# The maxima's rows of the attention stack: three DMAs for both row tiles instead of six

## The chip, the cores and the metric

The kernel runs on one core of one Trainium2 chip. The metric is the device time of one execution in microseconds (us). Three runs of the kernel before gave 1207.92, 1214.93 and 1221.93 us; the median is 1214.93 us.

## What is computed

One transformer layer on `x` of shape (16, 512, 128): attention with 16 heads of width 8 and an ALiBi bias, then a mixture of eight experts (top 2) plus a shared one, each followed by a layernorm. The change lies in the attention's softmax:

```python
q = (x @ q_w + q_b).reshape(Bx, Tx, NH, HD).transpose(0, 2, 1, 3)
att = jnp.einsum('bhqd,bhkd->bhqk', q, k) * (1.0 / np.sqrt(HD))
att = att + build_alibi_bias(NH, Tx)[None]
att = jnp.where(causal[None, None], att, -jnp.inf)
att = jax.nn.softmax(att, axis=-1)
y = jnp.einsum('bhqk,bhkd->bhqd', att, v)
...
x = _layernorm(x + attention(x)); x = _layernorm(x + ffn(x))
```

## The kernel before, in words

**Two phases.** `attention` runs first, `experts` after it. The change is in `attention`, which takes the 16 sequences of the batch one after the other, as a software pipeline: in step n the unit work of sequence n runs beside the projections of sequence n+2, the maxima of n+1 and n+2, and the output work of n-1.

**The stack.** The scores of a head are a matmul over up to 64 rows of two tiles in SBUF, `qstack` and `kstack` (three buffers of each, 128 partitions, 8 slots of 512 columns). Partitions 0 to 63 are row tile 0, with the even heads, and 64 to 127 row tile 1, with the odd heads. In each row tile, rows 0 to 47 hold q or k cut into bf16 parts, rows 48 to 51 the bias, rows 52 to 54 (`MAX_ROW` and the two after it) minus the row's maximum, cut into three bf16 parts, and the last rows a mask. So the maximum is subtracted by the score matmul itself, and ScalarE takes the exponential straight from PSUM.

**How the maxima's rows are made.** `max_bank` (L601 to L608) computes the scores without the maxima's rows, 40 banks for a sequence, and VectorE reduces each bank (L921). After the last bank of a sequence VectorE gathers the result in `rowmax` (L930, L932). Then, in the last quarter of a step: job `m` transposes `rowmax` on TensorE (L524), ScalarE writes the first part into `mparts[:, 0, :]` (L664, raises `m_high`), and VectorE what is left into `mrest` (L852, raises `m_rest`); job `mr`: ScalarE writes the second part `mparts[:, 1, :]` (`m_high` again), VectorE the third, `mparts[:, 2, :]` (L857, `m_rest` again). `mparts` has 64 partitions, (head, query tile), 32 for each row tile, and 128 queries in a row.

**How they come to the stack.** SyncE waits for all of this (L499, L500) and then issues six DMAs (L504): for row tile 0 the three parts, then for row tile 1 the three parts. Each moves 32 source partitions of 256 bytes into one partition of `qstack`. Those of tile 0 raise `max_rows0`, those of tile 1 `max_rows1`.

**Who waits for them.** In the next step, TensorE's first score unit (unit 0, an even head) waits for `max_rows0` and unit 1 (an odd head) for `max_rows1`. Between the two stands one bank of maxima. ScalarE's job `m` of the next step waits for both before it writes over `mparts`.

**SyncE's order in a step** is fixed: load `xin` for three sequences ahead, load `xres`, 24 DMAs of `parts` into `qstack` and `kstack` (L469, for the sequence two ahead), one DMA that zeroes a piece of `x_sorted` (L493), the maxima's rows (L504), and the store of `x1T` (L509). TensorE's order is written out by `plan`: unit and bank of maxima in turn, with `pv` matmuls and the jobs in between; engines run it in that order.

Of the kernel before, what the change touches and what calls it, by code (L numbers as in the profile page):

```python
# [15 lines left out]
P = 128  # L16
B, T, C = 16, 512, 128
NH, HD = 16, 8
QT = T // P
# [7 lines left out]
PARTS = 3  # L27
ROW_TILES, ROWS, SLOTS = 2, 64, 8
# [316 lines left out]
def attention(nc, io, dram, keep):  # L345

    with ExitStack() as ctx:
# [6 lines left out]
        def sem(name):  # L354
# [50 lines left out]
        names = """const_loaded masks_loaded late_loaded stack_rows_loaded0 stack_rows_loaded1 stack_rows_loaded2 const_ready unit_ready max_ready pv_ready xT_ps q_ps k_ps v_ps m_ps y_ps ynT_ps o_ps  # L405
            x1T_ps lg_ps exp_done xT_ready qk_high y_kept m_high ynT_ready x1T_ready max_taken rowmax_ready
            qk_split m_rest v_ready y_normed z_ready ln_done rstd_ready logits_kept zeros_set vaug_zeroed rows_zeroed masked qk_low res_biased x1_kept x_loaded0 x_loaded1 stats_passed maxima_passed exp_passed
            xres_loaded max_rows0 max_rows1 routed chosen prefix_ps placed places x_scattered ids_set routing_set x1T_stored shared_loaded""".split()
        S = {n: sem(n) for n in names}
        x_loaded = [S["x_loaded0"], S["x_loaded1"]]  # L410
        CONSTS, CONSTS_READY = 16 * 5, 5
# [14 lines left out]
        with nc.Block() as block:  # L426

            @block.sync
            def _(sp):
                def load(done, out, in_):  # L430
                    sp.dma_start(out, in_).then_inc(S[done], 16)

                load("const_loaded", ident[:], io["ident"])
                load("const_loaded", wq[:], io["q_w"])
                load("const_loaded", wkv_in[:], io["kv_w"])
                load("const_loaded", qb[:], io["q_b"].unsqueeze(1))
                load("const_loaded", kb[:], io["kv_b"][0:C].unsqueeze(1))

                def load_later():

                    for n in range(1, STACKS):
                        for stack, rows in ((qstack[n], io["qstack_rows"]), (kstack[n], io["kstack_rows"])):
                            for tile in range(ROW_TILES):
                                load(f"stack_rows_loaded{n}", stack[ROWS * tile + PROD:ROWS * (tile + 1), :, :].bitcast(U16),
                                     rows[tile])
                    load("late_loaded", wo[:], io["o_w"])
                    load("late_loaded", ob[:], io["o_b"].unsqueeze(0).to_broadcast([P, C]))
                    with nc.allow_non_contiguous_dma(reason="the router's weights transposed"):
                        load("late_loaded", gw[:], io["gate_w"].rearrange("e c -> c e"))
                    load("late_loaded", keep["rank"][:], io["rank"].unsqueeze(0).to_broadcast([P, NE]))  # L450
                    load("late_loaded", keep["before"][:].bitcast(U16), io["before"])
                    load("late_loaded", keep["ids"][:], io["ids"])

                def load_stack(st):

                    buffer, done = st.stack(2), stack_loaded[st.stack(2)]
                    if st.number + 2 >= STACKS:
                        sp.wait_ge(S["unit_ready"], st.at(2 - STACKS, SEQ_UNITS, SEQ_UNITS))
                    for part in range(PARTS):
                        for w, (stack, order) in enumerate(((qstack[buffer], Q_PARTS), (kstack[buffer], K_PARTS))):  # L460
                            if part < 2:
                                sp.wait_ge(S["qk_high"], st.at(2, 4, 2 * part + w + 1))
                            else:
                                sp.wait_ge(S["qk_low"], st.at(2, 2, w + 1))
                            for n in range(len(order)):
                                for tile in range(ROW_TILES):
                                    if order[n] == part:
                                        row = ROWS * tile + HD * n
                                        sp.dma_start(stack[row:row + HD, :, :],  # L469
                                                     parts[tile * HD * SLOTS:(tile + 1) * HD * SLOTS, w, part, :]) \  # L470
                                            .then_inc(done, 16)

                def body(st):
                    if st.has(3):
                        if not st.first(3) and (st.every or st.number + 3 >= 2):

                            sp.wait_ge(S["xT_ps"], st.at(1, 1, 1))
                        sp.dma_start(xin[st.par(3)][:], io["x"][bass.ds(st.number + 3, 1)]
                                     .rearrange("b (i p) c -> p (b i) c", p=P)).then_inc(x_loaded[st.par(3)], 16)
                    if st.chained():  # L480
                        if not st.first(-1):
                            sp.wait_ge(S["z_ready"], st.at(-2, 1, 1))
                        sp.dma_start(xres[:], io["x"][bass.ds(st.number - 1, 1)]
                                     .rearrange("b (i p) c -> p (b i) c", p=P)).then_inc(S["xres_loaded"], 16)
                    if st.has(2):
                        load_stack(st)
                    if st.has(0):

                        if st.first(0):
                            sp.wait_ge(S["zeros_set"], 1)  # L490
                        chunk, turn = divmod(st.number * CHUNKS, B)
                        rows = CSLOT * P * CHUNKS // B
                        sp.dma_start(dram["x_sorted"][chunk][turn // CHUNKS * rows:(turn // CHUNKS + 1) * rows, :]  # L493
                                     .rearrange("(n p) c -> p n c", p=P),
                                     zeros[:].unsqueeze(1).to_broadcast([P, rows // P, RW])).then_inc(S["rows_zeroed"], 16)
                    if st.first(2):
                        load_later()
                    if st.has(1):
                        sp.wait_ge(S["m_rest"], st.at(1, 2, 2))  # L499
                        sp.wait_ge(S["m_high"], st.at(1, 2, 2))  # L500
                        for tile in range(ROW_TILES):
                            for a in range(PARTS):
                                row = ROWS * tile + MAX_ROW + a
                                sp.dma_start(qstack[st.stack(1)][row:row + 1, :, :].rearrange("a u (i t) -> a (u i) t", t=P),  # L504
                                             mparts[tile * SLOTS * QT:(tile + 1) * SLOTS * QT, a, :]) \
                                    .then_inc(S[f"max_rows{tile}"], 16)
                    if st.chained():
                        sp.wait_ge(S["x1T_ready"], st.at(-1, 1, 1))
                        sp.dma_start(dram["x1T"][st.number - 1], x1T[:]).then_inc(S["x1T_stored"], 16)  # L509

                steps(sp, body)
                load("shared_loaded", keep["shared_in"][:], io["w_in"][:, NE, :, :])
                load("shared_loaded", keep["shared_down"][:], io["w_down"][:, NE, :, :])
                sp.wait_ge(S["shared_loaded"], 32)
                sp.wait_ge(S["rows_zeroed"], 16 * B)
                sp.wait_ge(S["x1T_stored"], 16 * (B - 1))

            @block.tensor
            def _(pe):
# [91 lines left out]
                def unit(st, g, u):  # L611

                    n = UNITS * g + u
                    if n < ROW_TILES:
                        pe.wait_ge(S[f"max_rows{n}"], st.at(0, 48, 48))
                    if n >= SB or not st.first(0):
                        pe.wait_ge(S["exp_done"], st.at(0, SEQ_UNITS, n - SB + 1))
                    q, ks = qstack[st.stack(0)], kstack[st.stack(0)]
# [43 lines left out]
            def _(act):  # L662
# [3 lines left out]
                def job(st, name):  # L666
# [16 lines left out]
                    elif name == "m":  # L683
                        act.wait_ge(S["m_ps"], st.at(1, 1, 1))
                        if not st.first(1):
                            act.wait_ge(S["max_rows0"], st.at(0, 48, 48))
                            act.wait_ge(S["max_rows1"], st.at(0, 48, 48))
                        copy(mparts[:, 0, :], misc[0:NH * QT, 0:P], "m_high", scale=-1.0)
                    elif name == "mr":
                        act.wait_ge(S["m_rest"], st.at(1, 2, 1))  # L690
                        copy(mparts[:, 1, :], mrest[:], "m_high")
                    elif name == "yn":
                        act.wait_ge(S["ynT_ps"], st.at(-1, 1, 1))
                        if not st.first(-1):
                            act.wait_ge(S["x1T_stored"], st.at(-2, 16, 16))
                        copy(ynT[:], misc[:], "ynT_ready")
                    elif name == "x1t":
                        act.wait_ge(S["x1T_ps"], st.at(-1, 1, 1))
                        copy(x1T[:], misc[:], "x1T_ready")
# [1001 lines left out]
```

## Time and profile before

| what | us |
|---|---|
| median of three runs | 1214.93 |
| profiled execution, its own time | 1221.95 |
| its span, first to last instruction | 1220.2 |
| attention phase, about | 0 to 760 |
| expert phase, about | 760 to 1220 |
| TensorE busy | 1049.4 (86%) |
| VectorE busy | 826.3 (68%) |
| ScalarE busy | 730.3 (60%) |
| GpSimd busy | 695.8 (57%) |

The profile is one execution; times in its views count from its first instruction. In the timeline a row is: start, duration, engine, line of the kernel, operation, output and inputs, how many instructions are merged in the row, and in brackets how long the engine stood idle before it and what ended that wait. "SPq" is SyncE's queue: a row of it is the time in which it issues DMAs, not the time in which they move data.

### The profile page before, as it was taken

What the parts mean: (1) busy time and instruction counts of PE and PEld (TensorE: products, weight loads), DVE (VectorE), ACT (ScalarE), POOL (GpSimd) and SP (SyncE); (2) the same over time, 40 slices, a digit from 0 to 9 for tenths busy, and PEclk for the clock granted to TensorE, in tenths of its full rate; (3) what the DMA queues carried; (4) which work ended last, traced back from release to release, by engine and by line L of the source; (5) the groups of instructions that cost most, each with busy time, mean ns of one, the idle gap of its engine ahead of it and who ended that gap; (6) DMA issues with size and microseconds to landing.
All of it is one profiled execution on the core that took longest, in us unless ns stands there. A gap on an engine that the chain in (4) does not pass through costs nothing. (4 is left out here: it accounts for less than half of the span.)

```text
span 1220.2 us, 28794 instructions
## 1 busy us (share of the span) xinstructions
PE 1049.4 (86%) x9396; PEld 713.9 (59%) x9396; DVE 826.3 (68%) x2070; ACT 730.3 (60%) x1577; POOL 695.8 (57%) x1191
## 2 busy tenths in 40 slices
PE   1577989998989899888888986997999999999991
PEld 0243444444444444344344433787999999999871
DVE  2567788888888888898889832573433334666585
ACT  1116666666667665466666665445777777788542
POOL 1004444554555454377677775377888888788531
PEclk9958999999999998799999998998999999999996
DMA  5734334433453334155334222412223222445233
GB/s 94 77 46 73 59 76 85 73 66 75 77 83 69 73 74 75 44 90 100 78 93 88 59 59 68 191 35 59 79 75 79 74 79 83 116 134 142 89 111 91
DMA packets 124625, 100.42 MB, mean 82 GB/s; under 512 B 19936, under 2 KB 115430, under 8 KB 124034
## 3 DMA queue, kind: packets, MB, share of 16 engines
q1 hardware_dynamic: 114642, 76.49, 31.9%
q0 software_dynamic: 8704, 16.87, 4.2%
q10 hardware_dynamic: 1136, 5.23, 1.3%
q8 instruction: 81, 1.33, 0.5%
q14 instruction: 62, 0.51, 0.2%
HBM read 37.82 MB, written 35.79 MB: 60 GB/s over the span
## 5 line engine op out<-in xcount | busy, mean ns | idle before, releaser
L711 ACT ACTIVATE probs<-scores 128x512 f32<-128x512 f32 x640 | 346.7, 599 | 110.0 <-PE scores L624 108.5
L774 POOL TENSOR_SCALAR_AFFINE_SELECT probs<-probs 128x256 f32<-128x256 f32 (+1 forms) x640 | 235.6, 381 | 255.8 <-ACT probs L711 246.1
L601 PE MATMUL maxed<-kstack,qstack 52*128 52x128 bf16 (+3 forms) x1152 | 224.5, 300 | 70.3 <-DMA kstack<-parts 36.6
L624 PE MATMUL scores<-qstack,kstack 64*128 64x128 bf16 (+3 forms) x1024 | 238.9, 305 | 43.2 <-DMA qstack<-mparts 17.6
L1227 DVE TENSOR_TENSOR e_hid<-e_gate,e_up_ps 128x352 f32<-128x352 f32 (+2 forms) x192 | 107.5, 560 | 184.6 <-ACT e_gate L1506 159.7
L921 DVE TENSOR_REDUCE maxA<-maxed 128x4 f32<-128x512 f32 x256 | 165.5, 682 | 86.4 <-PE maxed L608 85.8
L640 PE MATMUL pv<-probs,vaug 128*32 128x512 f32 (+3 forms) x2048 | 200.1, 464 | 2.9 <-POOL probs L774 2.9
L921 DVE TENSOR_REDUCE maxB<-maxed 128x4 f32<-128x512 f32 x256 | 162.1, 680 | 4.5 <-PE maxed L608 4.4
L1601 POOL DMA_INDIRECT y_tokens<-e_raw,e_row_i x144 | 142.8, 991 | 37.7 <-issue 26.6
L624 PEld LDWEIGHTS scores<-qstack,kstack 64*128 64x128 bf16 x1024 | 75.9, 94 | 150.6 <-ACT probs L711 82.2
L606 PE MATMUL maxed<-causal,halves 64*128 64x256 bf16 (+1 forms) x640 | 160.0, 261 | 0.0
L1506 ACT ACTIVATE e_gate<-e_gate_ps 128x352 f32<-128x352 f32 (+2 forms) x192 | 95.2, 496 | 84.3 <-PE e_gate_ps L1403 47.2
L608 PE MATMUL maxed<-causal,halves 64*128 64x192 bf16 (+1 forms) x640 | 143.8, 228 | 0.0
L601 PEld LDWEIGHTS maxed<-kstack,qstack 52*128 52x128 bf16 x1152 | 75.2, 95 | 91.5 <-issue 40.0
L1468 PE MATMUL e_y_ps<-e_w_down,e_hT 128*128 (+1 forms) x864 | 120.0, 275 | 0.0
L1413 PE MATMUL e_gate_ps<-e_w_in,e_xT 128*128 x432 | 106.3, 354 | 5.0 <-POOL e_w_in L1548 5.0
L1468 PEld LDWEIGHTS e_y_ps<-e_w_down,e_hT 128*128 128x128 f32 (+1 forms) x864 | 107.8, 191 | 0.0
L1413 PE MATMUL e_up_ps<-e_w_in,e_xT 128*128 x432 | 93.5, 325 | 0.0
L921 DVE TENSOR_REDUCE maxC<-maxed 128x4 f32<-128x512 f32 x128 | 82.1, 682 | 0.5
L608 PEld LDWEIGHTS maxed<-causal,halves 64*128 64x128 bf16 x640 | 63.9, 101 | 23.6 <-issue 6.1
L1518 ACT ACTIVATE e_hT<-e_h_ps 128x384 f32<-128x384 f32 x144 | 70.7, 491 | 7.5 <-PE e_h_ps L1456 0.7
L1413 PEld LDWEIGHTS e_up_ps<-e_w_in,e_xT 128*128 128x128 f32 x432 | 74.1, 189 | 0.0
(189 smaller groups left out, 1839.6 us busy)
## 6 DMA issues: line engine op xcount, KB each, us to landing
qstack<-parts SPq DMA_DIRECT2D x192, 64.0 KB
kstack<-parts SPq DMA_DIRECT2D x192, 64.0 KB
x_sorted<-zeros SPq DMA_DIRECT2D x16, 580.5 KB, 10.2
e_xs<-x_sorted SPq DMA_DIRECT2D x144, 64.5 KB
e_raw<-y_tokens SPq DMA_DIRECT2D x64, 128.0 KB
xin<-in_x SPq DMA_DIRECT2D x16, 256.0 KB, 3.2
e_group_in<-x1T_all SPq DMA_DIRECT2D x16, 256.0 KB, 3.0
out<-e_raw SPq DMA_DIRECT2D x64, 64.0 KB
```

What stands on the lines that cost most here:

```text
L601: pe.matmul(bank[:, at:at + (k1 - k0) * P], q[rows, slot, i * P:(i + 1) * P], ks[rows, slot, k0 * P:k1 * P], start=first, stop=False, skip ...
L606: pe.matmul(bank[:, at:at + wide], halves[rows, 0, :], causal[rows, 0:wide], start=False, stop=False, skip_group_check=True)
L608: pe.matmul(bank[:, at + ROWS:at + wide], halves[rows, 1, :], causal[rows, 2 * P:P + ROWS + wide], start=False, stop=True, skip_group_chec ...
L624: last = pe.matmul(scores[st.at(0, SEQ_UNITS, n) % SB][:, col:col + width], ks[rows, slot, kt * P:(kt + 1) * P], q[rows, slot, kt * P:T], ...
L640: last = pe.matmul(pv[hh * VW:(hh + 1) * VW, kt * P:T], vaug[st.par(off)][:, kt, g * QUAD + hh, :], probs[g % 2][:, at * T + col:at * T + ...
L711: act.activation(probs[g % 2][:, u * T:(u + 1) * T], scores[st.at(0, SEQ_UNITS, UNITS * g + u) % SB][:], ACT.Exp).then_inc(S["exp_done"], 1)
L774: pool.affine_select(out=view, in_=view, compare_op=ALU.is_ge, fill=0.0, base=0, pattern=pattern, channel_multiplier=-1).then_inc(S["maske ...
L921: dve.tensor_reduce(out.rearrange("p a b -> p (a b)"), maxed[st.at(max_stage(n), MAXB, n) % MB][:].rearrange("p (j t) -> p j t", t=P), AX. ...
L1227: dve.tensor_tensor(hid[step % len(hid)][rows, 0:cols], gate[step % 2][rows, 0:cols], up_ps[step % 2][rows, 0:cols], ALU.mult).then_inc(S[ ...
L1413: done = pe.matmul(bank[:, 0:F], xT[n % len(xT)][:, x_part, :], w_in[:, e, w, w_part, :].rearrange("p a f -> p (a f)"), start=m == 0, stop ...
L1468: done = pe.matmul(y_ps[:, 0:C], hT[n % 2][0:fw, j * P:(j + 1) * P], w_down[0:fw, e, j, :].rearrange("p a c -> p (a c)"), start=j == 0, st ...
L1601: pool.indirect_dma_start(out=dram["y_tokens"][n // CSLOT], out_offset=bass.IndirectOffsetOnAxis(ap=row_i[:, n:n + 1], axis=0), in_=ys[:, ...
```

## The change

The two row tiles' rows for one part are written by one DMA: its destination is the two partitions `MAX_ROW + a` and `MAX_ROW + a + 64`, its source all 64 partitions of `mparts[:, a, :]`. SyncE waits for each part by itself: the first two for `m_high` at one and two, the third for `m_rest`. There is one semaphore, `max_rows`, which reaches 48 for each sequence when all three have landed; TensorE waits for it at unit 0, and unit 1 has no wait of its own.

```diff
                     if st.has(1):
-                        sp.wait_ge(S["m_rest"], st.at(1, 2, 2))
-                        sp.wait_ge(S["m_high"], st.at(1, 2, 2))
-                        for tile in range(ROW_TILES):
-                            for a in range(PARTS):
-                                row = ROWS * tile + MAX_ROW + a
-                                sp.dma_start(qstack[st.stack(1)][row:row + 1, :, :].rearrange("a u (i t) -> a (u i) t", t=P),
-                                             mparts[tile * SLOTS * QT:(tile + 1) * SLOTS * QT, a, :]) \
-                                    .then_inc(S[f"max_rows{tile}"], 16)
+                        for a in range(PARTS):
+                            row = MAX_ROW + a
+                            if a < 2:
+                                sp.wait_ge(S["m_high"], st.at(1, 2, a + 1))
+                            else:
+                                sp.wait_ge(S["m_rest"], st.at(1, 2, 2))
+                            sp.dma_start(qstack[st.stack(1)][row:row + ROWS + 1:ROWS, :, :]
+                                         .rearrange("a u (i t) -> a (u i) t", t=P), mparts[:, a, :]) \
+                                .then_inc(S["max_rows"], 16)
...
-                    if n < ROW_TILES:
-                        pe.wait_ge(S[f"max_rows{n}"], st.at(0, 48, 48))
+                    if n == 0:
+                        pe.wait_ge(S["max_rows"], st.at(0, 48, 48))
...
                         if not st.first(1):
-                            act.wait_ge(S["max_rows0"], st.at(0, 48, 48))
-                            act.wait_ge(S["max_rows1"], st.at(0, 48, 48))
+                            act.wait_ge(S["max_rows"], st.at(0, 48, 48))
```

SyncE, at the end of one step and the start of the next, before and after (an xN row is N like DMAs in a row):

```order
-L504 DMA qstack<-mparts 1x32x128 [waits m_high,m_rest]
-L504 DMA qstack<-mparts 1x32x128 x5
-L509 DMA x1T_all<-ynT 128x512 [waits x1T_ready]
```

```order
+L505 DMA qstack<-mparts 2x32x128 [waits m_high] x2
+L505 DMA qstack<-mparts 2x32x128 [waits m_rest]
+L510 DMA x1T_all<-ynT 128x512 [waits x1T_ready]
```

Six DMAs behind one pair of waits have become three, each behind its own wait; what stands around them is the same.

TensorE, where a step begins (the L577 rows are the last job of the step before; L624 is a score unit, L601 to L608 a bank of maxima), before:

```order
L577 MATMUL misc<-gw,ynT 128x8 [waits x1T_ready]
L577 MATMUL misc<-gw,ynT 128x8 x3
L624 MATMUL scores<-qstack,kstack 128x512 [waits exp_done,max_rows0]
L601 MATMUL maxed<-kstack,qstack 128x512 [waits max_taken]
L606 MATMUL maxed<-causal,halves 128x128
L608 MATMUL maxed<-causal,halves 128x64
L624 MATMUL scores<-qstack,kstack 128x512 [waits exp_done,max_rows1]
```

and of the change:

```order
L578 MATMUL misc<-gw,ynT 128x8 [waits x1T_ready]
L578 MATMUL misc<-gw,ynT 128x8 x3
L625 MATMUL scores<-qstack,kstack 128x512 [waits exp_done,max_rows]
L602 MATMUL maxed<-kstack,qstack 128x512 [waits max_taken]
L607 MATMUL maxed<-causal,halves 128x128
L609 MATMUL maxed<-causal,halves 128x64
L625 MATMUL scores<-qstack,kstack 128x512 [waits exp_done]
```

The instructions stand in the same order; the wait of unit 1 is gone and unit 0 waits for all the rows.

## Rows read from the trace of the kernel before

**Rows 1.** The page, busy time of each engine over the span.
```profile
PE 1049.4 (86%) x9396; PEld 713.9 (59%) x9396; DVE 826.3 (68%) x2070; ACT 730.3 (60%) x1577; POOL 695.8 (57%) x1191
```

**Rows 2.** Windows, one attention step each, the last the experts; columns as headed.
```profile
core 0: us, PE busy (x) PEld busy (x) DVE busy (x) ACT busy (x) POOL busy (x), PEclk, DMA share, GB/s
332.85:373.39 40.54, 36.48 (x404) 18.84 (x403) 35.24 (x77) 27.51 (x54) 20.12 (x47) 1.00 0.45 76
...
551.33:593.15 41.82, 36.90 (x403) 18.95 (x403) 36.22 (x77) 27.40 (x54) 30.54 (x58) 1.00 0.47 90
593.15:636.51 43.36, 38.41 (x403) 19.49 (x403) 36.23 (x77) 27.55 (x54) 30.54 (x58) 0.96 0.39 88
...
760.00:1220.00 460.00, 421.57 (x3014) 400.10 (x3012) 249.74 (x838) 287.97 (x727) 315.50 (x382) 0.96 0.34 97
```

**Rows 3.** Waits of TensorE, 84 to 760 us: us in total, times, longest us.
```profile
PE scores L624 <- DMA qstack<-mparts: 17.6, 20, 1.9
...
PE maxed L601 <- DMA kstack<-parts: 9.8, 5, 4.9
```

**Rows 4.** Timeline around one change of sequence: the parts, the DMAs, the units.
```profile
326.77 0.27 ACT L664 ACTIVATE mparts<-misc 64x128 bf16<-64x128 f32 x1 [0.63 <-PE misc L524]
...
328.06 0.30 ACT L664 ACTIVATE mparts<-mrest 64x128 bf16<-64x128 f32 x1
...
328.69 0.27 DVE L857 TENSOR_TENSOR mparts<-mrest,mparts 64x128 bf16<-64x128 f32 x1
...
328.99 3.74 SPq L504 DMA_DIRECT2D qstack<-mparts  x6
...
332.85 0.39 PE L624 MATMUL scores<-qstack,kstack 64*128 64x512 bf16 x1
...
334.03 0.39 PE L624 MATMUL scores<-qstack,kstack 64*128 64x512 bf16 x1 [0.70 <-DMA qstack<-mparts]
```

**Rows 5.** Timeline, TensorE: two units 1 with another releaser named.
```profile
374.62 0.39 PE L624 MATMUL scores<-qstack,kstack 64*128 64x512 bf16 x1 [0.76 <-DVE maxA L921]
...
415.21 0.39 PE L624 MATMUL scores<-qstack,kstack 64*128 64x512 bf16 x1 [0.76 <-DVE maxA L921]
```

**Rows 6.** Timeline, TensorE: units 0 and 1 of the sequence before that of rows 4.
```profile
291.56 0.39 PE L624 MATMUL scores<-qstack,kstack 64*128 64x512 bf16 x1
293.45 0.39 PE L624 MATMUL scores<-qstack,kstack 64*128 64x512 bf16 x1 [1.41 <-DMA qstack<-mparts]
```

**Rows 7.** DMA, 329 to 333.6 us (40 slices of 0.115 us): the six DMAs alone.
```profile
GB/s 0 0 0 0 0 0 0 0 0 0 29 41 2 0 0 0 49 23 0 0 0 27 43 2 0 0 0 52 20 0 0 0 27 43 2 0 0 0 49 23
DMA packets 288, 0.05 MB, mean 11 GB/s; under 512 B 288, under 2 KB 288, under 8 KB 288
...
q1 hardware_dynamic: 288, 0.05, 5.3%
```

**Rows 8.** DMA, 340 to 357 us: the loads of `parts` (8x8 pieces of 1 KB each).
```profile
DMA packets 1224, 1.13 MB, mean 67 GB/s; under 512 B 132, under 2 KB 1223, under 8 KB 1223
...
q1 hardware_dynamic: 1223, 1.12, 50.5%
```

**Rows 9.** Timeline, SyncE and TensorE: the boundary with the shortest notice, and a slow issue.
```profile
122.61 3.77 SPq L504 DMA_DIRECT2D qstack<-mparts  x6
...
125.80 0.39 PE L624 MATMUL scores<-qstack,kstack 64*128 64x512 bf16 x1 [0.44 <-DMA qstack<-mparts]
...
674.65 4.76 SPq L504 DMA_DIRECT2D qstack<-mparts  x6
```

**Rows 10.** Waits of SyncE's queue, 291.56 to 332.85 us.
```profile
SPq L500 <- ACT mparts L664: 12.5, 1, 12.5
```

**Rows 11.** Timeline, TensorE: the first bank of maxima of the sequence two ahead.
```profile
365.34 0.39 PE L601 MATMUL maxed<-kstack,qstack 52*128 52x512 bf16 x1 [1.27 <-DMA kstack<-parts]
```

**Rows 12.** Windows, stretches at half clock behind a change of sequence (columns as rows 2).
```profile
455.70:462.50 6.80, 6.37 (x36) 2.06 (x33) 3.66 (x8) 2.92 (x5) 1.74 (x4) 0.50 0.39 117
...
595.60:599.00 3.40, 3.40 (x24) 1.46 (x20) 0.97 (x3) 1.49 (x4) 0.52 (x3) 0.50 0.48 143
```

More of the change, by code:

```diff
@@ L407, in attention @@
             qk_split m_rest v_ready y_normed z_ready ln_done rstd_ready logits_kept zeros_set vaug_zeroed rows_zeroed masked qk_low res_biased x1_kept x_loaded0 x_loaded1 stats_passed maxima_passed exp_passed
-            xres_loaded max_rows0 max_rows1 routed chosen prefix_ps placed places x_scattered ids_set routing_set x1T_stored shared_loaded""".split()
+            xres_loaded max_rows routed chosen prefix_ps placed places x_scattered ids_set routing_set x1T_stored shared_loaded""".split()
         S = {n: sem(n) for n in names}
```

## The prediction

> **What bounds the kernel now.** I read the page first: TensorE is busy 86% of the span, 18 points more than any other engine [rows 1], so a change that only touches DMAs can pay only where TensorE stands still for one. Then the windows by sequence [rows 2]: an attention step takes 40.5 to 43.4 us with TensorE busy 36.5 to 38.4 us, so about 4 us of each step are idle; the 460 us of the experts have nothing of the change in them. Then TensorE's waits within the attention [rows 3]: the largest single cause is `qstack<-mparts`, the DMAs that are changed: 17.6 us over 20 waits. Two more waits, 0.76 us each, carry the name of a VectorE reduction [rows 5], but they stand at unit 1 and fit the same pattern as their neighbours: 374.62 and 415.21 are each a unit 1. So the wait for the maxima's rows costs 17.6 + 2 x 0.76 = 19.1 us over 16 changes of sequence, 1.2 us each.
>
> How one of them comes about is in the timeline [rows 4]. The three parts are made at 326.77 + 0.27 = 327.04, 328.06 + 0.30 = 328.36 and 328.69 + 0.27 = 328.96. SyncE has then been waiting for 12.5 us at this place (the sequence before: [rows 10]) and issues six DMAs from 328.99 on, in 3.74 us, one every 0.62 to 0.63 us. The last is begun at about 332.12. Unit 1 starts at 334.03, so a DMA is of use 1.90 us after its issue began. Unit 0, which needs only the first three, starts at 332.85 without a wait. Unit 1 waits 0.70 us. ScalarE, VectorE and GpSimd live on what TensorE gives them here.
>
> **What the change does, part by part.**
>
> *Issue.* Three DMAs stand where six stood. The first is begun at about 327.1, the second at 328.4, 0.6 us before the third part is there, the third at about 329.0. The last of the transfers is so issued at 329.0 instead of 332.12: 3.1 us earlier. That comes from the number alone; that the first two are begun early takes only 1.2 us more off the queue ahead of the third, since all three must have landed. SyncE is free 3.1 us earlier for the store of `x1T` and the loads of `xin` and `xres`; none of these is waited for within the step, so I give that nothing, and if their cover went they would cost nothing either, being earlier.
>
> *Landing.* Each new DMA moves 64 pieces of 256 bytes into two partitions instead of 32 pieces into one. How many DMA engines share it decides its time. The six old ones show 288 packets [rows 7]: 48 each, 32 with data and 16 small ones that report completion, so all 16 engines take two pieces each. The loads of `parts`, whose destination has 8 rows of 8 pieces, show 132 packets under 512 bytes beside 1,091 larger ones of the queue's 1,223 [rows 8]: 64 to 7.7, that is about 8 completions for a DMA of 64 pieces, so 8 engines. The outer dimension of the destination seems to set the number, and the new one is 2 x 32: two engines with 32 pieces each, and the same two for all three DMAs. A packet of the old DMAs took 0.053 x 16 x 4.6 us / 288 = 13.5 ns, and one of `parts`, four times as large and with its queue full, 0.505 x 16 x 17 us / 1223 = 112 ns. So 30 more pieces on an engine cost from 0.4 us (13.5 ns) to 3.4 us (112 ns). I take 0.4 to 0.9 us, because the pieces have the size and the source of rows 7 (112 ns by a quarter of the bytes would be 28 ns). The third DMA is then of use 1.90 + 0.4 to 0.9 = 2.3 to 2.8 us after its issue, at 331.3 to 331.8, and unit 0 wants it at 332.85. At the boundary with the shortest notice, 122.61 to 125.80 - 0.44 = 125.36, there are 2.75 us [rows 9]: just enough.
>
> The Trainium skill ("DMA: Bandwidth & Descriptors", section on why a DMA increments its semaphore by 16) states the rule in full: the number of engines is the largest up to 16 that divides the slowest dimension, other than one, of both access patterns, and the lowest-numbered engines are taken. By that rule the six old DMAs run on 16 engines and the three new ones on 2, which would make each new transfer slower; the trace agrees as far as the 16 and the 8 go, and no row here shows a transfer on 2.
>
> *The waits.* With the rows landed before unit 0, both waits go: unit 0's, and unit 1's, whose place is filled by nothing, since VectorE, ScalarE and the banks are ready there. What is saved is 19.1 us if it isn't given back. For that I compare two steps. From unit 0 at 291.56 to unit 0 at 332.85 are 41.29 us, with a wait of 1.41 at unit 1 [rows 4, 6]; the next step takes 40.54 us with a wait of 0.70 [rows 2]. The difference is 0.75 us against 0.71 in the waits: a wait at this place goes into the length of the step in full. What would be late next is the stack of the sequence two ahead, for which TensorE waits 1.27 us later in the step [rows 11]; but those loads are begun behind unit 1 in the same step (after xT, q and its first part), so they move forward with it.
>
> *The sum.* In the profiled execution, 1221.95 - 19.1 = 1202.9 us. That execution lies 7 us above the median of the runs shown. It had groups of six issues that took longer than 3.74 us, such as 4.76 us [rows 9], five in all by about 0.9 us each, and unit 1 waits longer behind them; another execution need not have so many. I take off half of these 4.3 us and get 17 us: 1214.93 - 17 = **1198 us**, 1.4% less.
>
> *Clock.* At 595.6 the granted clock goes to half (0.50) for 3.4 us, just behind the unit 1 that had waited [rows 12]; that step takes 43.36 us and the one before 41.82 [rows 2], so such a stretch costs 1.5 us. There are five of them soon after a change of sequence, at 455.7, 510.3, 595.6, 680.9 and 718.5 (two of the five stand in rows 12). They may go with the waits, up to 7.5 us; I don't count them in the forecast, but the low end of the range has them.
>
> **Rivals.**
>
> *Given back.* The wait goes but a limit behind it takes its place: the stack's loads, 9.8 us of waits [rows 3, 11], or VectorE at 35.24 of 40.54 us [rows 2]. The result would be 0 to 5 us less than the median, 1210 to 1215 us. Against it speaks the comparison of steps; for it, that this shows one step with more wait, not one with none. Chance 17%.
>
> *Two engines are too few: slower.* The place is unit 0, which now waits for the last byte of all rows. The first slices with traffic in rows 7 begin 1.15 us after the first issue, so the pieces of the first new DMA flow from about 328.3 on. If the 96 pieces go one behind the other on each of the two engines, unit 0 starts at 328.3 + 96 p + 0.5, p being the time of a piece. It decides from where this is past 332.85 + 0.70 = 333.55, at p = 50 ns. At 112 ns it is 339.6, 6.7 us late, less the 1.2 us of today: 5.5 x 16 = 88 us slower, 1303 us. Midway, at 80 ns, 3.6 - 1.2 = 2.4, x 16 = 38 us slower, 1253 us. For it speaks that nothing shows a DMA of this form; against it the 13.5 ns. It is the case that the skill's rule of two engines leads to, if pieces are slow. Chance 6%.
>
> *Half of it.* The rows land between the old `max_rows0` and unit 1: p near 30 to 45 ns, or short notice as in rows 9. Unit 0 then waits up to 0.5 us at some boundaries and 8 to 12 us are won: 1203 to 1207 us. Chance 17%.
>
> *It doesn't do what it says.* SyncE might come late to the first part; with 12.5 us of waiting there [rows 10] it doesn't, and the gain rests on the third DMA anyway. I fold that into the first rival.
>
> **How the numbers follow.** The forecast has a chance of 60%, 1190 to 1203 us. The measurement of this kernel tells about 1% from no change, 12 us. Faster by more than that: the forecast, and a fourth of "half of it", 0.60 + 0.05 = 0.65. Within 1%: the rest of "half of it" and nearly all of "given back", 0.28. Slower: the two engines, and a little for what I don't see, 0.07. The low end is 1214.93 - 19.1 - 7.5 = 1188 us; the high end takes in "half of it" and most of the ways of "given back", 1212 us.
>
> **What would show it.** Right: three SyncE issues from 0.1 us behind the first part on, spaced by the parts; no wait of a score unit for `qstack<-mparts`; a quiet step of 39.8 us instead of 40.5; completion packets of 2 for each DMA (66 packets, not 80). "Half of it": a wait at unit 0 under 0.6 us. "Two engines": a wait at unit 0 above 1 us at every boundary. "Given back": no such wait, but steps of 40.5 us still, and more under `kstack<-parts` or VectorE. The forecast is wrong if pieces into the two partitions cost over 50 ns each, or if the quiet step doesn't shorten.

## The result

| kernel | median us | lowest to highest | runs |
|---|---|---|---|
| before | 1216.36 | 1207.92 to 1221.93 | 4 |
| the change | 1181.84 | 1176.10 to 1191.74 | 4 |

The ratio is 0.9737, with a 95% interval of 0.9687 to 0.9787: 32 us less by the ratio, 34.5 between the two medians. Forecast were 17 us less (1198 us, in a range of 1188 to 1212); the sign was right, the size was half of what came. Three more comparisons of the same two kernels gave 0.9703, 0.9706 and 0.9715. The last of them is from a chip where the whole takes 7% longer; its attention is as long as elsewhere, but what follows the last score matmul takes 552.5 us there in the profile of the change, and 469.1 in its first profile, so a ratio of such a chip makes a gain in the attention a little smaller than it is. Two of the change's six executions in that comparison were in a slower state that every kernel has now and then, and the median and ratio given for it leave them out.

**The profile after.** TensorE is busy for nearly as long as before, 1038 us against 1049 [rows 1], in a span that is 41 us shorter:

```profile
span 1178.9 us, 28715 instructions
...
PE 1037.9 (88%) x9396; PEld 711.1 (60%) x9396; DVE 825.1 (70%) x2070; ACT 727.3 (62%) x1577; POOL 694.9 (59%) x1191
```

TensorE's waits in the attention, 80 to 740 us (us in total, times, longest), which answer to [rows 3]: `qstack<-mparts` is gone from the list, and `kstack<-parts`, 9.8 us before, is 5.6 us.

```profile
PE scores L625 <- ACT probs L711: 17.4, 19, 1.8
PE maxed L602 <- DVE maxB L921: 17.0, 15, 4.2
PE e_x_ps L1355 <- DVE e_hid L1123: 6.0, 1, 6.0
PE maxed L602 <- DMA kstack<-parts: 5.6, 6, 1.2
```

The same change of sequence as in [rows 4], in the timeline: the first DMA begins 0.03 us behind the first part, the third (in the merged row of three; it begins at 312.78) 0.03 us behind the third part. Unit 0 starts at 316.59 and unit 1 0.32 us behind it.

```profile
310.37 0.27 ACT L665 ACTIVATE mparts<-misc 64x128 bf16<-64x128 f32 x1 [1.03 <-PE misc L525]
...
310.67 2.61 SPq L505 DMA_DIRECT2D qstack<-mparts  x3
...
311.66 0.30 ACT L665 ACTIVATE mparts<-mrest 64x128 bf16<-64x128 f32 x1
...
312.47 0.28 DVE L857 TENSOR_TENSOR mparts<-mrest,mparts 64x128 bf16<-64x128 f32 x1
...
316.59 0.39 PE L625 MATMUL scores<-qstack,kstack 64*128 64x512 bf16 x1
316.91 0.37 PE L625 MATMUL scores<-qstack,kstack 64*128 64x512 bf16 x1
```

What the transfers do from 311.80 to 314.20 us (40 slices of 0.06 us), against [rows 7]: each is a train of 9 slices at up to 38 GB/s, 0.5 us, where an old one was three slices of 0.115 us.

```profile
GB/s 4 21 34 38 34 34 38 38 30 0 0 0 0 0 0 0 0 0 0 0 0 0 13 26 34 38 34 38 34 38 17 0 0 0 0 17 21 34 34 34
DMA packets 165, 0.04 MB, mean 17 GB/s; under 512 B 165, under 2 KB 165, under 8 KB 165
...
q1 hardware_dynamic: 165, 0.04, 7.6%
```

A packet took 0.076 x 16 x 2.4 us / 165 = 17.7 ns; 32 of them on each of two engines are 0.5 to 0.6 us. The steps, against [rows 2]: the quiet one is 1 us shorter, not 0.7; the last row is the experts, 460 us again (from the last score matmul to the end are 469.1 us, and 472.5 before).

```profile
core 0: us, PE busy (x) PEld busy (x) DVE busy (x) ACT busy (x) POOL busy (x), PEclk, DMA share, GB/s
316.59:356.18 39.59, 36.29 (x403) 18.76 (x403) 35.16 (x77) 27.39 (x54) 20.13 (x47) 1.00 0.46 76
525.01:566.00 40.99, 37.98 (x403) 19.32 (x403) 36.29 (x77) 27.39 (x54) 30.59 (x58) 0.96 0.50 94
...
719.00:1178.90 459.90, 420.86 (x3018) 399.40 (x3018) 251.63 (x841) 288.26 (x729) 315.97 (x384) 0.97 0.34 97
```

So the mechanism is the one forecast, and some 15 us came on top. The experiments ask where from. Three candidates stood at the outset: A, only the landing counts, and a wait costs more than the profile shows; B, TensorE's clock falls less often; C, SyncE is free earlier. D was formed on the way, from step 0.

### The profile page after: what moved, and what is told of

Its sections match the earlier page's. It is cut to its first block and busy times, and to the rows that moved or that the text cites. A ratio compares the mean times of both kernels' runs of the same rounds, so it can differ in the third digit from the quotient of the medians.

```text
span 1178.9 us, 28715 instructions
## 1 busy us (share of the span) xinstructions
PE 1037.9 (88%) x9396; PEld 711.1 (60%) x9396; DVE 825.1 (70%) x2070; ACT 727.3 (62%) x1577; POOL 694.9 (59%) x1191
## 5 line engine op out<-in xcount | busy, mean ns | idle before, releaser
L625 PE MATMUL scores<-qstack,kstack 64*128 64x128 bf16 (+3 forms) x1024 | 234.4, 303 | 20.4 <-ACT probs L711 17.4
L641 PE MATMUL pv<-probs,vaug 128*32 128x512 f32 (+3 forms) x2048 | 196.4, 457 | 2.9 <-POOL probs L774 2.9
L609 PEld LDWEIGHTS maxed<-causal,halves 64*128 64x128 bf16 x640 | 63.7, 101 | 21.9 <-issue 6.3
L607 PEld LDWEIGHTS maxed<-causal,halves 64*128 64x128 bf16 x640 | 62.3, 98 | 20.2 <-issue 3.8
```

The source lines that it names most:

```text
L607: pe.matmul(bank[:, at:at + wide], halves[rows, 0, :], causal[rows, 0:wide], start=False, stop=False, skip_group_check=True)
L609: pe.matmul(bank[:, at + ROWS:at + wide], halves[rows, 1, :], causal[rows, 2 * P:P + ROWS + wide], start=False, stop=True, skip_group_chec ...
L625: last = pe.matmul(scores[st.at(0, SEQ_UNITS, n) % SB][:, col:col + width], ks[rows, slot, kt * P:(kt + 1) * P], q[rows, slot, kt * P:T], ...
L641: last = pe.matmul(pv[hh * VW:(hh + 1) * VW, kt * P:T], vaug[st.par(off)][:, kt, g * QUAD + hh, :], probs[g % 2][:, at * T + col:at * T + ...
```

## Experiments

"Half clock" below is the sum of the stretches in which the granted clock was 0.5 and which began between 84 and 760 us, from the profile of each run; a long stretch that every profile has from about 60 to 90 us isn't in it. A step runs from one unit 0 to the next, so it holds the wait of its own unit 1 and, at its end, that of the next unit 0.

**One: merged, but begun late.**

```diff
+                        sp.wait_ge(S["m_rest"], st.at(1, 2, 2))
+                        sp.wait_ge(S["m_high"], st.at(1, 2, 2))
                         for a in range(PARTS):
                             row = MAX_ROW + a
-                            if a < 2:
-                                sp.wait_ge(S["m_high"], st.at(1, 2, a + 1))
-                            else:
-                                sp.wait_ge(S["m_rest"], st.at(1, 2, 2))
```

> Three merged DMAs, but SyncE waits for all three parts before the first of them, as the kernel before does. The last is begun 1.25 us behind the third part instead of at once. Theory A (what counts is only that all rows land before unit 0 wants them, 3.9 us behind the third part in a quiet step): landing at about 3.4 us, so as the change, 1182 to 1187 us, with short waits at the few boundaries that give under 3 us of notice. Theory B (the gain beyond the removed 19 us is TensorE's clock, which falls less often when the wait is gone): the same time, and as few stretches at half clock as the change has. Theory C (it is SyncE, free earlier for the stores and loads behind): SyncE is free 1.3 us later than in the change, of the 3 us it gained, so about 40% of the excess of 14 us is lost, 1188 us.

Measured: 1190.41 us, ratio 0.9754 (0.9715 to 0.9793), beside 0.9703 (0.9659 to 0.9747) of the change in the same comparison. That is 3 us above what A and B forecast and 2 above C's 1188. Its profiled execution took 1180.81 us, the fastest of its six. A quiet step is 39.58 us, that of the change:

```profile
316.72:356.30 39.58, 36.32 (x403) 18.78 (x403) 35.15 (x77) 27.38 (x54) 20.12 (x47) 1.00 0.46 77
524.41:564.98 40.57, 36.71 (x403) 18.86 (x403) 36.14 (x77) 27.39 (x54) 30.50 (x58) 1.00 0.50 93
```

Unit 0 waited at two boundaries, the ones with short notice (0.46 and 0.65 us). Beginning each DMA early is worth about 1 us of waits, merging the rest; the two intervals overlap, so whether the 0.5% between this kernel and the change is real isn't settled.

**Two: six DMAs, begun early, in the order of the parts.**

```diff
-                        for tile in range(ROW_TILES):
-                            for a in range(PARTS):
+                        for a in range(PARTS):
+                            if a < 2:
+                                sp.wait_ge(S["m_high"], st.at(1, 2, a + 1))
+                            else:
+                                sp.wait_ge(S["m_rest"], st.at(1, 2, 2))
+                            for tile in range(ROW_TILES):
                                 row = ROWS * tile + MAX_ROW + a
```

> Six DMAs as before, each on 16 engines, but in the order of the parts, the two of a part begun when that part is made. The last is begun 0.6 us behind the third part instead of 3.1 us. Theory A: rows of both row tiles are there 2.5 us behind the third part, before unit 0: as the change, 1180 to 1186 us. Theory B: the same. Theory C: SyncE is free 0.6 us later than in the change, 1182 to 1186 us. If the merging itself mattered (fewer completions, less traffic), this stays well above, 1195 us or more.

Measured: 1191.86 us, ratio 0.9766 (0.9718 to 0.9813). That is 6 us above the forecast of all three theories. The last DMA begins 1.1 to 1.2 us behind the third part in half of the sequences and up to 2.0 us in the others, not 0.6, because the four DMAs of the first two parts are still being issued; that is still early enough. Quiet steps are 39.58 us, and waits for the rows came to 0.9 us in two pieces. So the steps don't need the merging; either half of the change takes nearly all of the waits away, and four fifths of the gain came with either. Its half clock was 37.5 us. It waited 10.9 us for `kstack<-parts`, 6.0 of them in step 0, where the change waits 0.8: here D began.

**Three: the wait put back, twice as long.** Six small DMAs ahead of the third one hold it back:

```diff
+                            if a == 2:
+                                ...
+                                for i in range(6):
+                                    sp.dma_start(spare[:, 16 * i:16 * (i + 1)], mparts[:, 0, 16 * i:16 * (i + 1)]).then_inc(S["spare_rows"], 16)
                             sp.dma_start(qstack[st.stack(1)][row:row + ROWS + 1:ROWS, :, :]
```

> The change, with six small DMAs into a spare tile begun between the second and the third of the maxima's DMAs, so that the third is begun 3.75 us late and lands about 5.8 us behind the third part. Unit 0 wants it at 3.9 us: a wait of 1.9 us in a quiet step, up to 3 at others, 35 us in all on TensorE. Theory A with the wait at its shown length: 1182 + 35 = 1217 us. Theory A with a restart cost beside each wait (0.25 us each, read off quiet steps): 1221 us. Theory B: more than that, 1225 to 1235 us, with half-clock stretches behind most changes of sequence.

Measured: 1254.81 us, 70 us above the change (1185.05) on the same chip. TensorE's waits, 84 to 760 us, and two steps:

```profile
PE scores L632 <- DMA qstack<-mparts: 38.6, 16, 3.5
```

```profile
352.27:396.60 44.33, 39.43 (x402) 19.64 (x403) 35.23 (x76) 27.65 (x53) 20.19 (x46) 0.92 0.41 70
585.18:627.73 42.55, 36.78 (x402) 18.88 (x403) 36.13 (x76) 27.29 (x53) 30.51 (x58) 1.00 0.47 89
```

Each step ends with a wait at the next unit 0, of 1.97 us in the first and 1.91 in the second. In the second the clock stayed at 1.00: against 40.57 without a wait (above) it is 1.98 us longer, the length of the wait and 0.07. In the first stand 6.8 us at half clock, most of them behind the wait that came before it (0.92 in the mean of the step): 44.33 against 39.58, 4.75 us, of which 1.97 are the wait and 2.7 the clock. Half clock was 102.4 us in all. So a wait at unit 0 costs its length, and a long one mostly brings the clock down behind it, which costs more than the wait. Neither price of A was enough; B's range (1225 to 1235) was too low as well. The two prices do nearly give the 70 us: 38.6 for the waits, and at 0.40 us for each of the 64 us of half clock more than in the mean of the ten profiles with hardly a wait (39 us, below) 25, so 64; the loads of step 0 (nine and ten, below) add 4.

**Four: the wait put back at its old length.** As three, with four spare DMAs; on a chip where the kernel before takes 1297.12 us, so by ratios.

> As the run with six spare DMAs, with four: the third of the maxima's DMAs is begun 2.5 us late, so that unit 0 waits about 0.7 us in a quiet step and 18.6 us in all (38.6 us read in the profile with six, less 1.25 us at each of 16 changes), which is what the kernel before waited in all (19.1 us). If a wait costs its shown length: 1185 + 18.6 = 1204 us. If the whole difference between the kernel before and the change comes of the wait and what it brings with it (restart, clock), this lands where the kernel before is, 1216 to 1221 us; by the slope of the run with six (70 us for 38.6) it is 1185 + 34 = 1219 us. Then half-clock stretches of 45 us or more in the attention.

Measured: 1289.38 us, ratio 0.9919 (0.9888 to 0.9949), between the forecast by the length alone (1204 of 1220 us, 0.987) and that of the kernel before. The waits sum to 16.0 us; those of the kernel before, profiled again on this chip, are 13.6 us under its own name and 3.0 under VectorE's, 16.6 us. With nearly the same wait this kernel is 10 us (7 to 15) faster. One difference is where it waits:

```profile
333.10 0.39 PE L632 MATMUL scores<-qstack,kstack 64*128 64x512 bf16 x1 [0.61 <-DMA qstack<-mparts]
333.10 0.60 PE L609 MATMUL maxed<-kstack,qstack 52*128 52x512 bf16 x2
...
333.42 0.37 PE L632 MATMUL scores<-qstack,kstack 64*128 64x512 bf16 x1
```

Once unit 0 goes, unit 1 follows 0.32 us behind it, before unit 0's 0.39 us are over and although a bank of maxima stands between them: matmuls of the two row tiles overlap. In the kernel before unit 1 followed after 1.18 us [rows 4], so 0.86 us late, and the profile shows 0.70 as its wait. The step tells the whole: 40.28 us here with 0.63 of wait at its end (39.58 + 0.70), 40.54 there with 0.70 (39.58 + 0.96). A wait at unit 0 costs 0.07 us more than is shown and one at unit 1 0.26 us more, of which the late start explains 0.16. It isn't one step's luck: 16 steps at full clock in the two profiles of the kernel before, worked out in the same way, give 0.25 to 0.35. Over 16 changes of sequence it is 4 us. Of the 10 us between the two kernels this and the 0.6 us of wait explain 3 to 4. The rest isn't traced; the profile of this one has 6.8 us less half clock, worth 3 us at most.

**Five: SyncE as busy as before, rows as early as in the change.** Three spare DMAs behind the third one; same chip as four.

```diff
                                 .then_inc(S["max_rows"], 16)
+                            if a == 2:
+                                ...
+                                for i in range(3):
+                                    sp.dma_start(spare[:, 16 * i:16 * (i + 1)], mparts[:, 0, 16 * i:16 * (i + 1)]).then_inc(S["spare_rows"], 16)
```

> The change, with three small spare DMAs begun behind the third of the maxima's DMAs: SyncE is as busy as before the change and comes to the store of x1T and to the loads of xin and xres 1.9 us later, while the rows land as early as in the change. If SyncE's freedom is worth something (theory C): 1190 us or more. If only the landing counts: 1185 us within 3, no wait for the maxima's rows. In step 0 it also tells whether the loads of the stack are served fast (under 18.5 us) with merged DMAs alone or whenever few small DMAs were issued: the spare ones run on 16 engines as the old six.

Measured: 1267.97 us, ratio 0.9751 (0.9701 to 0.9800), within the interval of the change. No wait for the rows, quiet steps of 39.58 us, as long as in the change. That is what speaks against C. The total doesn't settle it: it is 29 us under the kernel before, where the change gained 32 to 36, and by its ratio, with 1220 us for the kernel before, it is 1190 us, the threshold that was set for C. Some 4 us of that are step 0, which is D's (below). Between this and four lie 21 us for 16.0 us of wait. But half clock is 54.6 us here, as much as with the wait: the clock isn't decided by these waits alone. And step 0 is slow, 39.55 us, with a wait of 4.9 us for `kstack<-parts`.

**Six: the kernel before again**, same chip as four.

> The kernel before once more, for a second profile: 1216 to 1222 us, quiet steps of 40.5 to 40.6 us with a wait of 0.70 to 0.76 us, half-clock stretches of about 55 us in the attention (theory B), against 34 and 48 in the two profiles of the change. If step 0 takes 39 us or more and its loads 21.5 us or more again, the 8 us of step 0 in the first pair of profiles belong at least in part to the form of the DMAs; if it takes 33 to 35, they were chance.

Measured: 1293.10 us, ratio 0.9968 (0.9937 to 1.0000). Half clock 61.4 us; step 0 takes 41.69 us. In step 12 the rows had 4.8 us from the third part to unit 0 instead of 3.8, unit 1 didn't wait, and that step takes 39.48 us; the one behind it takes 41.38, with a wait of 1.03 us at unit 1 and 0.61 at the next unit 0, so 0.26 more than shown again.

**Seven and eight: the change again, and once more.**

> The changed kernel once more, for a second profile and for the comparison with the others on one chip. All theories: 1182 us within 6. What differs in the first profile pair without a wait for the maxima's rows behind it should be read here again: if the first step (sequence 0) is again 8 us shorter than before, and the loads of the stack in it are again served in under 19 us, that belongs to the change; if not, it was chance of that execution.

> The changed kernel a third time, as the reference of this chip. Ratio to the kernel before of 0.970 to 0.975. Theory D: loads of step 0 under 20.5 us again.

Measured: 1185.05 us, ratio 0.9703 (0.9659 to 0.9747), and 1184.36 us, ratio 0.9706 (0.9640 to 0.9772). Half clock 47.8 and 34.1 us. Step 0 of the second profile took 37.72 us and its loads 20.2, not the under 19 that were asked for, so this run by itself doesn't confirm the 33 us of the first profile. Two steps of the second profile differ in the clock alone:

```profile
162.62:203.55 40.93, 37.97 (x402) 19.31 (x402) 35.35 (x77) 27.44 (x54) 20.20 (x47) 0.96 0.45 75
244.47:284.05 39.58, 36.60 (x402) 18.92 (x402) 35.15 (x77) 27.29 (x54) 20.18 (x47) 1.00 0.40 81
```

One stretch of 3.4 us at half clock in the first: 1.35 us, 0.40 for each us at half clock. In the steps of sequences 10 to 13 the same stretch costs 0.42 us (40.99 against 40.57).

These four steps have two lengths, whatever the kernel: without a wait and at full clock 40.57 us, or 39.41. They go with one VectorE instruction, `k_rest` (L833 in the change), which takes 2.44 us in the long steps and 0.68 in the short ones. All four are short in experiments five and six; of the other twelve profiles five have one short step and seven none. Why it takes the longer or the shorter time no run here shows, but it moves a profile by up to 4.6 us, and a step may only be compared with one of its own kind.

**Nine and ten: which form goes ahead of step 0.** The change with only the first sequence's rows as six DMAs, and the reverse, in which the first line reads `if not st.first(1):` (the counts that TensorE and ScalarE wait for follow).

```diff
+                            if st.first(1):
+                                for tile in range(ROW_TILES):
+                                    at = ROWS * tile + row
+                                    sp.dma_start(qstack[st.stack(1)][at:at + 1, :, :].rearrange("a u (i t) -> a (u i) t", t=P),
+                                                 mparts[tile * SLOTS * QT:(tile + 1) * SLOTS * QT, a, :]) \
+                                        .then_inc(S["max_rows"], 16)
+                                continue
```

> The change, but the rows of the first sequence alone go as six DMAs (two for a part, begun when the part is made); all others are merged. In every profile so far the loads of the stack in step 0 took 17.6 to 20.2 us where the DMAs ahead of them were the three merged ones alone (3 of 3), and 21.8 to 22.8 us where there were small DMAs on 16 engines among them (6 of 6), and TensorE waited 5 us more for them. Theory D (the form of the DMAs ahead sets how fast the loads of step 0 are served): 21.5 us or more here, a wait of 4 to 6 us for kstack in step 0, a step 0 of 38 us or more, and 3 to 5 us on the whole, 1188 to 1190 us where the change has 1185. Theory E (chance): step 0 as in the change.

> The reverse: the first sequence's rows by three merged DMAs, all others by six, the two of a part begun when it is made. Theory D: loads of step 0 in 17.5 to 20.5 us and a wait for kstack under 3 us, the whole 1185 to 1188 us. Theory E: no rule; step 0 as in any of the others.

Measured: 1189.58 us (0.9735, 0.9656 to 0.9814) and 1187.76 us (0.9720, 0.9653 to 0.9786): the totals don't separate them from the change. The profiles do. Step 0 of nine (first row and wait), of ten, and of the change a third time, each from its own profile:

```profile
84.47:123.66 39.19, 32.50 (x331) 15.18 (x330) 29.73 (x55) 25.43 (x49) 16.36 (x40) 0.81 0.42 68
```

```profile
115.36 0.62 PE L609 MATMUL maxed<-kstack,qstack 52*128 52x512 bf16 x2 [4.94 <-DMA kstack<-parts]
```

```profile
84.70:119.26 34.56, 31.15 (x331) 14.52 (x328) 30.57 (x56) 26.05 (x50) 16.65 (x41) 0.88 0.36 67
```

```profile
84.41:117.58 33.17, 30.86 (x332) 14.54 (x327) 29.63 (x55) 25.11 (x49) 16.36 (x40) 0.87 0.38 73
```

From first to last 1 KB piece the 24 loads of the stack in step 0 took 22.0 us in nine and 18.0 in ten. Over all profiles: 17.6 to 20.2 us in the seven in which only merged DMAs had gone ahead, 21.8 to 22.8 us in the seven with small DMAs on 16 engines among them. D holds: the form of a few small DMAs, run 10 us earlier, sets how fast these loads are served. Why is not known. It isn't the same elsewhere: in steps 4 and 8 the loads take 17.9 to 19.2 and 16.8 to 17.6 us in the six profiles in which SyncE has only merged DMAs to issue there, each begun early (the change, nine, eleven), and 20.8 to 22.1 and 19.3 to 21.0 us in the rest. Among these are experiment one, merged but late, and five, merged and early with spare ones behind; so there it goes with when SyncE is free. TensorE waits for none of these loads.

**Eleven and twelve: a try for a better version,** with the change beside it; on the chip of the third comparison. On SyncE the DMA that zeroes `x_sorted` goes ahead of the stack's loads.

```diff
-                    if st.has(2):
-                        load_stack(st)
                     if st.has(0):
...
                         sp.dma_start(dram["x_sorted"][chunk][turn // CHUNKS * rows:(turn // CHUNKS + 1) * rows, :]
                                      .rearrange("(n p) c -> p n c", p=P),
                                      zeros[:].unsqueeze(1).to_broadcast([P, rows // P, RW])).then_inc(S["rows_zeroed"], 16)
+                    if st.has(2):
+                        load_stack(st)
```

> A try for a better version: the change, with the DMA that zeroes a piece of x_sorted begun ahead of the loads of the stack instead of behind them, in the 6 us in which SyncE waits for q's first part. If the waits for kstack that are left (5.6 us over the attention in the first profile) come of the zero writes sharing engines with the last loads, up to 5 us less, 1179 us; if the loads are served as slowly without it, no change within 0.3%.

> The changed kernel as the reference on this chip: ratio to the kernel before 0.970 to 0.975. Loads of the stack in step 0 under 20.5 us (theory D).

Measured: 1266.14 us, ratio 0.9712 (0.9676 to 0.9747), and 1265.67 us, ratio 0.9715 (0.9656 to 0.9775). No difference. TensorE's waits for `kstack<-parts` are 5.3 us in the one and 10.0 in the other, but single steps make that difference. The loads of step 0 took 18.7 and 19.9 us. It does not beat the change.

## Why the prediction was half right

**What bounds it, the landing, the issue: right.** The third DMA begins at the third part and its pieces take 15 to 18 ns each, near the lower bound that was taken; its train ends 1.6 us behind the issue, and unit 0 waits nowhere, not even at short notice. The rule on the number of engines (the Trainium skill, "DMA: Bandwidth & Descriptors", section on why a DMA increments its semaphore by 16) holds by this trace: 64 pieces and 2 completions for a DMA (the small packets of the run fell by 1440, as 16 x (6 x 16 - 3 x 2) says). "Two engines are too few", "half of it" and "given back" are out.

**The sum: wrong, "what is saved is 19.1 us if it isn't given back".** That took each wait at the length shown, and put the clock and the loads of step 0 at nothing. Four things stand in the place of the one term, and they give most of the 32 to 36 us that the ratios say:

| term | us | from |
|---|---|---|
| waits as shown | 17 to 19 | [rows 3, 5], experiment six (16.6) |
| a wait at unit 1 costs 0.26 more than shown, x 16 | 4 | experiment four |
| half clock outside step 0, 47 us in the mean of three profiles with 16 us or more of such waits, 32 in the ten with under 3, x 0.3 to 0.4 | 4 to 6 | all but three |
| step 0: loads served faster, and its clock | 4 to 5 | nine and ten |
| sum | 29 to 34 | |

With step 0 the half clock is 57 and 39 us. The 0.3 to 0.4 is an estimate between the 0.12 and 0.40 read in seven. The profiles agree with the sum: from the first unit 0 to the end of the last score matmul the kernel before takes 663.2 and 657.6 us, and the change 624.9 to 633.8 in four profiles, 32.4 less in the mean. 6.2 of these lie in step 0, 2.0 of them the wait terms.

**The comparison of two steps** was the place where it could have been seen. 41.29 and 40.54 us have a wait of 1.41 and 0.70 [rows 2, 4, 6]; the difference gives the cost of more wait, and a constant part of each wait drops out of it. The profile had the constant: unit 1 begins 1.18 us behind unit 0, of which 0.70 is called waiting.

**The clock** was left out of the forecast and put into the low end at 7.5 us. It belonged in the forecast at its mean, with a caveat that stays: single profiles with under 3 us of these waits have 23.9 to 54.6 us of half clock, those of the kernel before 54.6 and 61.4, so the share is a mean over executions. With long waits (three) the link is plain.

**That the loads "move forward with it"** held in all steps but the first: in step 0 the kernel before waits 4.92 us for them, and the change 0.56 to 3.46 in four profiles. The prediction counted that wait among the 9.8 us of [rows 3] and didn't ask for it by itself.

**Taking off 2 us** for slow issues moved the forecast the wrong way, and its reason didn't hold: in experiment six the waits are 2.5 us less, but the slow groups are five again; at steps 10 and 12 unit 0 came late (5.0 and 4.8 us behind the third part), and unit 1 waited 0.06 us and not at all.

## What to carry to other kernels

A wait's price is the step without it, not the idle time shown. Where two matmuls on different row tiles would overlap, look at how far behind its neighbour the waiting one starts; if no step without the wait is in the trace, the range has to reach up as well as down. When several transfers feed one wait, order them by when their data is made and count what stands behind the last datum: that, not the number of transfers or engines, decided the waits here.

## What was not expected of the hardware

A wait of 1.9 us of TensorE at the start of a step was mostly followed by a fall of the granted clock to half for 3.4 or 6.8 us (at 13 of 16 boundaries of experiment three, with waits of 1.9 to 3.5 us). A step with such a wait and 6.8 us at half clock was 4.75 us longer, and 1.98 where the clock held. Short waits of 0.6 to 0.8 us were mostly not followed by one. 64 pieces of 256 bytes from SBUF to two partitions ran at 15 to 18 ns each on two engines, with an issue of 0.53 us on SyncE. The same 24 loads of 64 KB took from 17.6 to 22.8 us in step 0, and which of the two it was went with the form of DMAs that had ended 10 us before, in 14 of 14 profiles; the reason is open.
